# One fixed order for groups 2 to 7 of a graph-convolution kernel on one core

## What is computed

```python
h = jnp.maximum(_layernorm(x, axis=-1), 0.0)
x = x + _L0_gnn_ref(h, adj, L0_gnn_b1, adj, L0_gnn_b2)
```

## Time and profile before

| | us |
|---|---|
| median of 3 runs (467.45 to 469.01) | 468.46 |
| the profiled execution | 466.62 |
| its span, first to last instruction | 464.8 |
| PE busy | 421.0 (91%) |
| DVE busy | 395.5 (85%) |
| ACT busy | 307.8 (66%) |
| POOL busy | 223.0 (48%) |
| mean granted TensorE clock | 0.984 |

### The profile page before, as it was taken

How to read it: one execution, slowest core, us unless ns; L and a number is a source line. 1 busy time by engine, 2 the same in 40 slices (tenths; PEclk the granted TensorE clock), 3 DMA queues, 4 the chain that set the end, 5 groups by cost and what they waited for, 6 DMA issues and landing times.

```text
span 464.8 us, 7615 instructions
## 1 busy us (share of the span) xinstructions
PE 421.0 (91%) x2220; PEld 176.1 (38%) x2220; DVE 395.5 (85%) x682; ACT 307.8 (66%) x657; POOL 223.0 (48%) x937
## 2 busy tenths in 40 slices
PE   0663899998989999899999999999999999999996
PEld 0121343334333444344444444444434444444432
DVE  5999898978999999999999999999999848844463
ACT  3979687969787799657967888677965752014300
POOL 2526656373838338624646373744565343315200
PEclk9995999999999999999999999999999999999999
DMA  8991000068404590076504590069304400430026
GB/s 308 362 411 56 1 0 1 36 237 276 179 0 186 189 352 0 2 271 229 223 3 181 185 359 1 29 245 322 131 0 183 182 1 0 183 157 25 0 104 259
DMA packets 19401, 68.21 MB, mean 147 GB/s; under 512 B 1824, under 2 KB 2464, under 8 KB 19360
## 3 DMA queue, kind: packets, MB, share of 16 engines
q1 hardware_dynamic: 19360, 67.73, 39.2%
HBM read 34.17 MB, written 33.55 MB: 146 GB/s over the span
## 4 chain that ended last, share of the span: by engine, by line
PE 42%; DVE 30%; ACT 12%; POOL 7%; issue 7%; DMA 1%; SPq 0%; POOLq 0%; DVEq 0%
PE ps L451 34%; DVE xs L1166 7%; DVE hl L1141 7%; DVE bn L1119 5%; ACT hl L677 4%; ACT hf L656 4%; ACT hl L665 3%; PE ps L457 3%; DVE hl L1150 3%; PE pm L506 2%; POOL nw L890 1%; DVE idx L1190 1%; DVE fv L1182 1%; PE pm L493 1%; PE pm L526 1%
## 5 line engine op out<-in xcount | busy, mean ns | idle before, releaser
L451 PE MATMUL ps<-hl,wh 128*128 128x512 f16 x896 | 268.7, 382 | 15.3 <-DVE wl L1325 11.3
L451 PE MATMUL ps<-hl,wl 128*128 128x512 f16 x448 | 170.6, 381 | 0.0
L451 PEld LDWEIGHTS ps<-hl,wh 128*128 128x128 f16 x896 | 83.7, 99 | 125.7 <-issue 22.0
L656 ACT ACTIVATE hf<-xs,nbias,rstd 128x1024 f32<-128x1024 f32 x64 | 79.2, 1237 | 24.6 <-POOL nbias L894 23.3
L1166 DVE SCALAR_TENSOR_TENSOR xs<-ps,sc,xs 128x1024 f32<-128x1024 f32 (+1 forms) x71 | 79.2, 1138 | 7.9 <-PE ps L457 7.9
L1141 DVE TENSOR_TENSOR hl<-hf,hl 128x1024 f16<-128x1024 f32 x64 | 77.3, 1211 | 6.8 <-ACT hl L665 6.6
L1150 DVE SCALAR_TENSOR_TENSOR hl<-ps,hl 128x1024 f16<-128x1024 f32 (+1 forms) x55 | 57.3, 1081 | 20.3 <-ACT hl L677 20.2
L677 ACT ACTIVATE hl<-ps 128x512 f16<-128x512 f32 x96 | 55.6, 593 | 22.4 <-PE ps L457 22.4
L665 ACT ACTIVATE hl<-hf 128x1024 f16<-128x1024 f32 x64 | 67.6, 1056 | 2.0
L908 POOL COPY gat<-hl 128x4 f16 x256 | 49.5, 245 | 32.7 <-DVE idx L1190 25.1
L1119 DVE BATCH_NORM_STATS2 bn<-xs 128x6 f32<-128x512 f32 x96 | 61.2, 677 | 4.4 <-DMA xs<-x_dram 4.3
(11 more groups left out here) (146 smaller groups left out, 523.2 us busy)
## 6 DMA issues: line engine op xcount, KB each, us to landing
xs<-x_dram SPq DMA_DIRECT2D x62, 512.0 KB, 7.4
out_dram<-xs SPq DMA_DIRECT2D x31, 1024.0 KB, 5.1
xs<-x_dram SPq DMA_DIRECT2D x4, 256.0 KB, 3.5
out_dram<-xs SPq DMA_DIRECT2D x4, 256.0 KB, 2.1
wt<-adj_t_dram SPq DMA_DIRECT2D x1, 256.0 KB, 10.5
b1r<-b_row_dram SPq DMA_DIRECT2D x1, 128.0 KB, 10.6
b2r<-b_row_dram SPq DMA_DIRECT2D x1, 128.0 KB, 11.4
cs<-consts_dram SPq DMA_DIRECT2D x1, 84.5 KB, 10.1
```

Source lines behind the costliest of these rows:

```text
L451: pe.matmul(bank(i, e), w[:, k, o], src, start=(k == 0 and w is wh and part == 0), stop=False)
L656: act.activation(hf[:, c % NHF], xs[:, n % NX, k], ACT.Relu, bias=nbias[:, n % RB, k:k + 1], scale=rstd[:, n % RB, k:k + 1], accum_out=s_a ...
```

## The change

In g > 1 all groups take one order, near that which g = 2 had. On TensorE the product with q1 comes after units 2 and 3 (before: 0 and 1) for g > 2; the means of the next group after units 4, 5 and 6, 7 (before: 2, 3 and 4, 5); `plain_rows` after unit 14 instead of 13. On ScalarE the h of `front(g, 0)` is made behind the first two `y_hi` of group g and no longer at the end of group g - 1. On VectorE, for g > 1, `top_a` and `top_b` stand behind the last `y_lo`, `top_c` and `top_d` behind the third row step; the residual steps of units 14 and 15 stand behind the last row step of the old group, ahead of `class_degrees`, where they began the next group (g > 2) or stood there already (g = 1). GpSimd's and SyncE's orders stay.

```diff
@@ TensorE
-                    if i == (2 if g < 3 else 0):
+                    if i == 2:
                         times_q1(g)
-                    if g == 2 and i in (4, 6):
+                    if g > 1 and i in (4, 6) and is_group(g + 1):
                         means(g + 1, i // 2 - 2)
-                    if g > 2 and i in (2, 4) and is_group(g + 1):
-                        means(g + 1, i // 2 - 1)
...
                     rows(*us[4:6])
-                    if g > 2:
-                        plain_rows(g + 1)
                     main(*us[6])
-                    if g in (1, 2):
+                    if g > 0:
                         plain_rows(g + 1)
                     main(*us[7])
@@ ScalarE: the branch of g > 2 is gone, that of g == 2 holds for all g > 1
-                elif g == 2:
+                else:
                     y_hi(*us[0][1:])
                     y_hi(*us[1][1:])
                     n = front(g, 0)
...
                     y_hi(*us[4][1:])
                     y_hi(*us[5][1:])
-                    means_copy(g + 1, 0)
+                    if to:
+                        means_copy(g + 1, 0)
                     root(FIRST[g] + 9)
                     make_h(n, 1)
                     y_hi(*us[6][1:])
                     y_hi(*us[7][1:])
...
                 make_h(n, 1)
-                if to and g > 1:
-                    n = front(g + 1, 0)
-                    make_h(n, 0)
-                    make_h(n, 1)
@@ VectorE: the branch of g > 2 is gone, that of g == 2 holds for all g > 1
-                elif g == 2:
+                else:
                     y_lo(*y[0])
                     y_lo(*y[1])
...
                     y_lo(*y[6])
                     y_lo(*y[7])
-                    top_a(g + 1)
-                    top_b(g + 1)
-                    top_c(g + 1)
-                    top_d(g + 1)
-                else:
-                    final(*unit(g - 1, 14)[1:])
-                    final(*unit(g - 1, 15)[1:])
...
                     if to:
                         top_a(g + 1)
                         top_b(g + 1)
...
                 end = [u[1:] for u in units(g, 2) + units(g, 3)]
                 rows_x(2 * g + 1)
...
+                if to:
+                    top_c(g + 1)
+                    top_d(g + 1)
                 mean_var(first + 10)
                 n = front(g, 2)
                 final(*end[0])
...
                 if to:
                     rows_w(2 * (g + 1))
-                if to:
+                    final(*unit(g, 14)[1:])
+                    final(*unit(g, 15)[1:])
                     class_degrees(g + 1)
                     inverse_degrees(g + 1)
                 h_lo(n, 1)
```

More of the change, by code:

```diff
@@ L813, in _ @@
                     y_hi(*us[7][1:])
-                    means_copy(g + 1, 1)
-                    n = front(g, 2)
-                    make_h(n, 0)
-                    make_h(n, 1)
-                else:
[L819 to L826, removed]
-                    if to:
[L828 to L832, removed]
                     if to:
@@ L836, in _ @@
                     make_h(n, 0)
-                    y_hi(*us[6][1:])
-                    y_hi(*us[7][1:])
                     make_h(n, 1)
@@ L1527, in _ @@
                         top_b(g + 1)
[L1528 to L1533, removed]
                 end = [u[1:] for u in units(g, 2) + units(g, 3)]
```

## The result

The changed kernel takes 476.61 us in the median (476.27 to 476.85, 4 runs), the kernel before 468.74 in the same comparison (467.45 to 469.07): a ratio of 1.0167, 95% interval 1.014 to 1.0195. It is 7.9 us slower where 12.8 were forecast, 476.6 where 481.3 was, inside the range. The sign and the places of the stalls were right, the size was six tenths.

What follows compares the result with a forecast made beforehand. TensorE was taken to bound the middle with hardly a gap, busy 50.37 of 51.00 us. Groups 2 to 6 added 1.45 + 2.77 + 3.34 + 3.30 + 1.9 = 12.8 us to 468.46, giving 481.3; range 474.0 to 486.5.

Steps and rivals of the forecast that it cites:

- (a): Group 2's row steps: with the search split they end at 188.85, so TensorE's 1.97 us wait for lw goes.
- (b): Unit 11's second bank, group 2: passes c and d delay the first residual step; TensorE waits 2.03 us, clock 0.08 us better.
- (c): Group 2's gather, 7.63 us: VectorE's sums wait 2.7, TensorE 1.13 at unit 15 and 0.4 at class counts; group +1.45.
- between none and three: VectorE's h subtractions meeting the gather, 1.06 us each: four groups move by -4.2 to +4.2 us.
- (d): Residual steps of units 14, 15 at old group's end: 0.54 us wait in group 3's unit 1 goes; later class degrees covered.
- Groups 3 to 5: Each takes group 2's order and lasts as long, 54.33 us: +2.77, +3.34 and +3.30 us.
- Group 6: No statistics, one batch's h: near 1.7 us at unit 11, 0.2 us at unit 15, gather 6.46 us; +1.9 us.
- Group 7: No search and no next group; GpSimd waits over 10 us in its later product with q1: 0.
- The first: Rival: only the bank stall at unit 11 comes, the gather is covered; +6.3 us, 474.8 us; chance 0.13.
- The prediction's other figure: Gather 1.17 us shorter in groups 2 to 5 if VectorE's waiting kept its subtractions out of it: 476.6 us.
- The second: Rival: VectorE 2.5 us ahead at unit 11's second bank, passes c and d fit, stalls go: 465.8 us; chance 0.06.
- The third: Rival: GpSimd's chain to q2 meets one more subtraction, 1.06 us in each of four groups: 485.5 us; chance 0.09.

Runs made afterwards that it cites:

- The split alone: The kernel before with only passes c and d moved behind the row steps in g > 1: 482.32 us, ratio 1.0292.
- putting the sums late: The changed kernel with the two sums over the gather behind unit 11's residual step instead of ahead of it: 472.94 us, ratio 1.0103.
- half: The changed kernel with the sums behind unit 11's residual step, pass c ahead of the row steps and pass d behind them: 471.06 us, ratio 1.0048.
- the search whole: The changed kernel with passes c and d put back ahead of the row steps in g > 1: 479.70 us, ratio 1.0235.
- the longer bank wait: The changed kernel with one more VectorE instruction, an unread maximum of about 0.3 us, behind pass d: 478.92 us, ratio 1.0236.

## Why the prediction was right, and where its size was off

**What bounds it, and (a): right.** The wait for lw is gone; the row steps took 190.63 - 188.31 = 2.32 us for 2.30.

**(b), the bank of unit 11: right.** From start to start TensorE lost 1.98 us in group 2 for 2.03 (the list shows 1.81 in each of groups 2 to 5). The residual step follows the mean and variance after 193.33 - 193.14 = 0.19 us, not 0.28, and TensorE goes on 1.29 us after its start, not 1.34. Counted from the group's start it goes on 0.21 us earlier than before (194.62 - 156.23 for 193.04 - 154.44), where 0.08 was forecast. The split alone, on the old order, gives the same 1.81 us.

**(c), the gather: the mis-sized term.** The sentence "From its new start both subtractions still fall in it, so I take 7.63" is where it failed. Both did fall in it, but on its first two sets of copies and not on its last, and it lasted 6.67 us. It began when forecast, 37.94 us into the group; with the 0.96 us less, and without the 0.2 us for the addition behind it, the sums waited 1.59 us, not 2.7. What TensorE felt of this is unit 15: it lost 0.07 us there, not 1.13. At the class counts it lost 0.43 us for 0.4, as forecast. So group 2 adds up to -0.21 + 0.07 + 0.43 = +0.29 us (measured +0.30) where the forecast had -0.08 + 1.13 + 0.4 = +1.45, and of the 1.15 us between them 1.06 are unit 15's. By the groups the forecast was 12.8 - 8.5 = 4.3 us too high: 1.15 to 1.3 us in each of groups 2 to 5, less 0.55 for group 6.

My bounds missed this for two reasons. They charged 1.06 us for each meeting wherever it falls, while the gathers above show the full price only where the last set is met. And "between none and three" is not -4.2 to +4.2 by that price: from two meetings to none in four groups it is -8.5, and by the two gathers of the earlier trace rows, 7.63 and 6.46 us, it is -4.7.

**(d), residual steps of units 14 and 15: right.** The 0.54 us in group 3's unit 1 went, and the product with q1 doesn't wait. That its later place is what makes this free was shown by moving the steps alone: 470.83 us.

**Groups 3 to 5 follow group 2: right.** 53.16, 53.04 and 53.09 us beside its 53.18. **Group 6: too small,** +2.45 for +1.9: the gather, taken at 6.46 us, lasted 7.56 there, the sums waited 3.98 us, and unit 15 waited 1.02 us, for which I had 0.2. So the same term was too large in four groups and too small in the fifth. **Group 7:** 53.3 us to the end of the span, as before.

**Rivals.** The first (only the bank stall, 474.8) came nearer to the number than the forecast, 1.8 us off against 4.7, but not wholly for its reason: the gather is not covered, and putting the sums late won 3.2 us by the groups. Still, what the gather cost TensorE, 0.5 us a group for 1.53, lies nearer to its nothing than to the forecast. The prediction's other figure, 476.6 for a gather that meets no subtraction, is the measured time by luck: both subtractions fell in the gather. The second failed as expected, since the residual step had 0.49 us of idle time where 2.5 were needed. The third: the meetings ahead of q2 were as many as in g = 2 before, and its wait stayed below 0.4 us.

The cause: the old order makes the last batch's h at the end of the group before, so that the means come early and VectorE can search in front of its last low parts. With the means two units later the search stands between the last low part and the first residual step, where VectorE has no slack. Group 2 of the kernel before had the late means and the whole search already, and its 1.97 us. Split or whole or half, TensorE waited 1.2 to 2.1 us there in groups 2 to 5 of every variant of the new order. That the later means, with the h ahead of them, open this gap was not tried by itself: it is what group 2 before and the trials of the split, the residual steps and the sums one by one leave.

## What to carry to other kernels

Before a step is moved in a hand-written order, follow the resource that it frees (here a bank, three units on) and the engine that it releases (here GpSimd's gather) to the next instruction that waits for each: splitting a late step moves a stall, it does not remove it, unless the two parts fall on two waits that both had slack. A group that already runs in the new order is the best price list for the others. Compare groups and not spans when the start varies by 2 us.

## What the runs showed of the hardware that was not expected

TensorE's clock falls behind an idle time of about 2 us in a busy stretch, but not always. With the search whole it fell behind 1.97 to 1.98 us in g = 3 to 5 and behind 2.64 us in g = 6, and kept 1.00 behind 1.97 us in g = 2. With the longer bank wait it fell behind 2.13 us in three groups of four and not behind 2.00 us. In the changed kernel's profile it fell neither behind its four waits of 1.81 us nor behind the one of 1.68. Where it falls it stands at the lower level for some 3 us, two matmuls take 1.06 us instead of 0.59, and about 1.4 us are lost. With the residual steps alone, the kernel before's own wait in group 2 did it too:

```profile
192.00:194.00 2.00, 1.60 (x6) 0.39 (x7) 1.21 (x5) 1.39 (x4) 1.77 (x13) 0.64 0.00 0
194.00:196.00 2.00, 2.00 (x6) 0.73 (x5) 2.00 (x3) 1.94 (x5) 1.42 (x6) 0.50 0.02 4
```

The kernel before has that wait (1.97 us), and this may be part of why its runs spread by 3 us and more; its one profile does not show the fall there. And a GpSimd chain of register loads and copies is hardly lengthened by the time for which VectorE holds up its copies, if that comes early: 6.67 us with two early meetings, 6.38 to 6.85 in three gathers with none, 7.63 with the second of two on the last set. That the loads go on meanwhile fits this, but the profile does not show the loads.
